# The projections of a second attention layer as products of rounded halves, with their weights streamed, in a fused two-layer kernel

## The chip, the cores and the metric

One core of one Trainium2 chip runs the whole program. The metric is the time of one execution on the device, in microseconds (us), of that core.

## The reference

Four batch rows of 512 tokens and width 256 pass through two layers, each a gated cross-attention and a gated feed-forward part. Only the second layer's attention matters here, cut from the reference:

```python
q = _split_heads(jnp.einsum('bnd,df->bnf', x, Wq))          # 16 heads of 64
kv = jnp.einsum('bmc,cf->bmf', context, Wkv)                # context 512 x 512
k, v = jnp.split(kv, 2, axis=-1)
nk = jnp.broadcast_to(null_kv[0], (b, HEADS, 1, DH))        # one null key for all
k = jnp.concatenate((nk, k), axis=-2)
attn = jax.nn.softmax(jnp.einsum('bhid,bhjd->bhij', q * scale, k), axis=-1)
out = jnp.einsum('bhij,bhjd->bhid', attn, v)
out = jnp.einsum('bnf,fd->bnd', out.transpose(0, 2, 1, 3).reshape(b, -1, INNER), Wout)
```

x is first normalised over its width; after the attention come a normalisation with scale and bias, the residual, and a mixture of eight experts of which each token uses two. All is in float32.

## The kernel before

The first layer fills the first third of the time, the second layer's attention (function `layer1`) the middle, the experts the rest. `layer1` walks over 32 groups, `i = 8 * b + p`: batch row b of four, and pair of heads p of eight (`PAIRS`). A group has four steps r = 0 to 3, one for each tile of 128 tokens or of 128 context rows. Every engine runs its own instructions in the order in which they are written, and semaphores join them.

In step (i, r) TensorE computes the scores of the next group (`scores(i + 1, r)`), transposes a quarter of this group's probabilities (`transpose_probs`, 8 transposes), and multiplies the quarter before it by the values (`weigh_values`). VectorE takes the row maxima of the new scores (`maxima`) and, one step later, divides the probabilities by their sums (`normalize`). ScalarE takes the exponentials (`exponentials`), copies the transposed probabilities out of PSUM (`keep_probs`) and the finished result (`keep_result`). The group's transposes start only when all four tiles of its probabilities are normalised (`p_ready`).

Into these steps a table, `slots`, puts further work, the fills. All fills share one PSUM bank, `MISC`, so a fill may start only when the one before it has been read out: `fill` waits for the reader's count, `misc_act` or `misc_dve`, and `read_fill` is that reader. The slot (i, r, 0) lies behind the scores and (i, r, 1) behind the transposes:

```python
        if 0 <= i + 2 < GROUPS:
            slots[i, 0, 0] = ("q", i + 2)
            slots[i, 1, 0] = ("k", i + 2)
```

A fill "q" projects the queries of a pair of heads (`project_queries`, 2 matmuls of 128x128 by 512 columns), "k" the keys (`project_keys`, 4 matmuls, two in step 1 and two in step 2), "v" a quarter of the values for half of the heads (`values`, 4 matmuls; 8 such fills for a batch row, in steps 3 of groups p = 0, 3, 4, 6, 7). "xT" transposes half of the next row's tokens (p = 5, in steps 2 and 3), "null" are the scores of the null key (p = 6, step 2, `null_scores`), "out" the output projection (p = 1, 2), "rT", "logits" and "prefix" belong to the choice of experts. `layer1` projects the keys and queries of groups 0 and 1 and the first values elsewhere; its own fills are 30 of q, 30 of k and 28 of v.

The projections are float32 matmuls. The scores are not: for groups 2 and later queries and keys are split when they are read out of PSUM into a part rounded to the format fp32r (`q_hi`, `k_hi`) and the remainder (`q_lo`, `k_lo`), and three fp32r matmuls, high by high, high by low and low by high, are added in PSUM. ScalarE rounds q, VectorE does the rest.

`wq`, `wk`, `wv` lie whole in SBUF, loaded once; the context of a batch row (`ctxT`) is loaded when the last keys of the row before are projected. The experts' weights will later stream into the SBUF buffers `w13_flat` and `w2_flat` of `Stream`; in the middle third these are empty until the last two groups. The trace calls the tiles of wq, wk, wv, ctxT and the experts' weights all `moe_w`, and xT `l_rows`. GpSimd adds a bias and a scale once per batch row and scatters rows for the experts.

## Time and profile before

| | |
|---|---|
| median of 3 runs | 1827.59 us (1826.96 to 1829.00) |
| the profiled execution's own time | 1830.33 us |
| its span, first to last instruction | 1828.6 us |
| mean granted clock of TensorE, as a share of 2.4 GHz | 0.983 |
| TensorE matmul busy, share of the span | 93% |
| VectorE, ScalarE, GpSimd busy | 65%, 57%, 21% |

Engines in the rows are PE (TensorE matmuls), PEld (its weight loads, which run beside them), DVE (VectorE), ACT (ScalarE), POOL (GpSimd) and SP (the queue that issues loads). A float32 matmul is two instructions in the trace. Matmuls are pipelined and their ends are modelled: the distance between starts is the cost of one, not its printed duration.

### The profile page before, as it was taken

To read this page: it belongs to the slowest core of one execution; us is meant where nothing else is said; L and a number is where in the kernel's file an instruction comes from. 1 tells how busy PE (TensorE), PEld (TensorE's weight loads), DVE (VectorE), ACT (ScalarE), POOL (GpSimd) and SP (SyncE) were. 2 spreads that over 40 slices of the span, in tenths; PEclk is the share of its full clock that TensorE was granted. 3 is DMA by queue.
4 is the path that set the end of the run, shared out by engine and by line. 5 is a ranking of instruction groups with operands and counts; after the bars stand their busy time and mean duration, and the time that the engine had idled before them with its cause. 6 is when DMAs were issued, how large, how long until landed. Compare 5 with 4: busy or idle time off the path is not lost.

```text
span 1828.6 us, 27461 instructions
## 1 busy us (share of the span) xinstructions
PE 1696.2 (93%) x9294; PEld 1082.1 (59%) x9294; DVE 1195.2 (65%) x2830; ACT 1045.7 (57%) x2160; POOL 375.5 (21%) x374
## 2 busy tenths in 40 slices
PE   5899998899799899999999999999998888999998
PEld 3455555455455345444554455444645788999997
DVE  3867876876778667555567457664676688666632
ACT  2467666666666656655555546555455466666621
POOL 2101110120011010000000000200021467777721
PEclk9899999999999999999999999999999899999999
DMA  3000000010003009200000000100001757777775
GB/s 104 1 24 1 1 24 1 1 28 3 1 1 138 2 2 347 73 24 1 1 1 23 1 1 1 58 2 1 13 25 56 227 148 218 214 210 198 218 230 161
DMA packets 121147, 127.10 MB, mean 70 GB/s; under 512 B 9904, under 2 KB 116400, under 8 KB 121008
## 3 DMA queue, kind: packets, MB, share of 16 engines
q1 hardware_dynamic: 113280, 116.68, 20.2%
q0 software_dynamic: 7152, 8.66, 2.6%
q8 instruction: 75, 1.23, 0.3%
q14 instruction: 64, 0.52, 0.1%
q10 hardware_dynamic: 576, 0.00, 0.0%
HBM read 96.46 MB, written 29.77 MB: 69 GB/s over the span
## 4 chain that ended last, share of the span: by engine, by line
PE 53%; DVE 5%; DVEq 1%; issue 1%; SPq 1%; ACT 0%; DMA 0%; POOLq 0%
PE psum L2497 8%; PE psum L1845 6%; PE psum L1716 6%; PE psum L1700 6%; PE psum L1722 5%; PE psum L1831 5%; PE psum L2515 4%; PE psum L1707 3%; PE psum L2472 3%; PE psum L1756 2%; PE psum L2482 1%; DVE moe_w_lo L2615 1%; DVE l_k_lo L2109 1%; DVE l_k_hi L2107 1%; PE psum L2454 0%
## 5 line engine op out<-in xcount | busy, mean ns | idle before, releaser
L1273 DVE TENSOR_REDUCE l_tile_max<-psum 128x1 f32<-128x512 f32 x512 | 342.1, 689 | 109.9 <-PE psum L951 108.2
L1121 ACT ACTIVATE l_probs<-psum 128x1024 f32<-128x1024 f32 x256 | 248.3, 1022 | 105.7 <-PE psum L963 102.0
L951 PE MATMUL psum<-l_kT,l_qT 128*128 128x512 f32 x512 | 238.3, 473 | 40.1 <-DVE l_tile_max L1273 36.8
L2049 DVE TENSOR_REDUCE l_row_max<-psum 128x2 f32<-128x1024 f32 x124 | 151.6, 1223 | 140.7 <-PE psum L1700 139.9
L2784 POOL TENSOR_TENSOR moe_w_lo<-moe_w,moe_w_hi 128x512 fp32r<-128x512 f32 x128 | 179.9, 1407 | 92.7 <-ACT moe_w_hi L2568 91.6
L951 PEld LDWEIGHTS psum<-l_kT,l_qT 128*128 128x128 f32 x512 | 98.0, 192 | 132.3 <-DVE l_tile_max L1273 111.7
L1888 ACT ACTIVATE l_probs<-psum,l_neg_max 128x512 f32<-128x512 f32 x248 | 167.2, 674 | 0.0
L963 PE MATMUL psum<-l_qT,l_kT 128*128 128x512 f32 x512 | 160.4, 397 | 1.7 <-ACT l_probs L1121 1.5
L1831 PEld LDWEIGHTS psum<-ident,l_probs 128*128 128x128 f32 x1024 | 120.5, 143 | 68.8 <-issue 53.1
L2599 ACT ACTIVATE moe_gate<-psum 128x256 f32<-128x256 f32 (+1 forms) x184 | 64.7, 352 | 158.7 <-PE psum L2497 98.5
L2497 PE MATMUL psum<-moe_xs_hi,moe_w_hi 128*128 128x256 f32 x512 | 148.0, 289 | 1.4 <-DVE moe_xs_lo L2625 1.4
L2497 PE MATMUL psum<-moe_xs_lo,moe_w_hi 128*128 128x256 f32 x512 | 146.3, 286 | 0.0
L2497 PE MATMUL psum<-moe_xs_hi,moe_w_lo 128*128 128x256 f32 x512 | 146.1, 285 | 0.0
L1831 PE MATMUL psum<-ident,l_probs 128*128 128x128 f32 x1024 | 136.3, 277 | 5.2 <-DVE l_probs L2063 3.9
L1845 PE MATMUL psum<-l_probsT,l_v_sb 128*64 128x512 f32 x512 | 140.6, 628 | 0.0
L978 PE MATMUL psum<-l_probs,l_v_ones 128*32 128x512 f32 x1024 | 138.7, 614 | 0.6 <-ACT l_probs L1121 0.6
L1886 ACT ACTIVATE l_null_p<-l_s_null,l_neg_max 128x1 f32<-128x1 f32 x248 | 71.4, 288 | 116.7 <-DVE l_neg_max L2051 116.4
L1926 ACT ACTIVATE l_probsT<-psum 128x1024 f32<-128x1024 f32 x128 | 130.4, 1019 | 5.7 <-PE psum L1831 5.7
L1716 PE MATMUL psum<-moe_w 128*128 128x512 f32 x240 | 119.0, 618 | 0.3 <-DVE router_work L545 0.3
L2063 DVE TENSOR_SCALAR l_probs<-l_probs,l_recip 128x512 f32<-128x512 f32 x248 | 110.0, 486 | 9.9 <-issue 0.4
L963 PEld LDWEIGHTS psum<-l_qT,l_kT 128*128 128x128 f32 x512 | 95.8, 189 | 29.4 <-ACT l_probs L1121 7.1
L1987 POOL TENSOR_TENSOR l_rows<-l_rows,l_ln_scale 128x256 f32<-128x256 f32 x12 | 9.8, 835 | 470.9 <-DVE l_rows L161 470.9
(361 smaller groups left out, 3278.6 us busy)
## 6 DMA issues: line engine op xcount, KB each, us to landing
moe_w<-in_moe_w SPq DMA_DIRECT2D x276, 256.0 KB, 4.6
moe_sorted_x<-l_null_cols SPq DMA_DIRECT2D x1, 17680.0 KB, 56.4
moe_xs<-moe_sorted_x SPq DMA_DIRECT2D x16, 272.0 KB, 2.9
moe_w<-in_ctx SPq DMA_DIRECT2D x8, 512.0 KB, 3.6
moe_w<-in_ctxT SPq DMA_DIRECT2D x4, 1024.0 KB, 5.7
moe_w<-in_wkv SPq DMA_DIRECT2D x2, 2048.0 KB, 15.7
x_resid<-in_x SPq DMA_DIRECT2D x4, 512.0 KB, 11.0
out_x<-x_resid SPq DMA_DIRECT2D x4, 512.0 KB, 4.4
```

The lines of the kernel that those rows point to most:

```text
L951: nc.tensor.matmul(bank(max_bank(m)), qT[:, q % SLOTS, h, t * P:(t + 1) * P], kT[:, q % SLOTS, h // 2, half * BANK:(half + 1) * BANK], sta ...
L963: last = nc.tensor.matmul(bank(2 * (n % 2) + i), kT[:, q % SLOTS, c, kt * P:(kt + 1) * P], qT[:, q % SLOTS, 2 * c + i, :], start=True, sto ...
L978: last = nc.tensor.matmul(bank(O_BANK)[32 * j:32 * j + 32, :], v_ones[:, q % SLOTS, kt, j, :], probs[:, (n + j // 2) % PT_RING, j % 2, :], ...
L1121: nc.scalar.activation(probs[:, n % PT_RING], wide(2 * (n % 2)), ACT.Exp, scale=SCALE).then_inc(exp_done, 1)
L1273: nc.vector.reduce_max(tile_max[:, q % 2, t, h, half:half + 1], bank(max_bank(m)), AX_X).then_inc(max_read, 1)
L1716: last = nc.tensor.matmul(bank(MISC), wk[:, c, p * P:(p + 1) * P], ctxT[:, c, :], start=(c == 0), stop=(c == s.CC - 1))
L1831: last = nc.tensor.transpose(bank(4 + j)[:, t * P:(t + 1) * P], probs[i % 2][:, t, j, kt * P:(kt + 1) * P], ident[:])
L1845: last = nc.tensor.matmul(bank(O_BANK)[j * DH:(j + 1) * DH, :], v_sb[:, kt, h * DH:(h + 1) * DH], probsT[:, m % 2, j, :], start=(kt == 0), ...
L1888: last = nc.scalar.activation(probs[i % 2][:, t, j, :], bank(2 * (t % 2) + j), ACT.Exp, bias=neg_max[:, t, j:j + 1], scale=SCALE, accum_ou ...
L2049: nc.vector.reduce_max(row_max[:, t, :], wide(2 * (t % 2)).rearrange("p (j m) -> p j m", j=2), AX_X)
L2497: last = nc.tensor.matmul(up_bank(k)[:, n * ROWS:(n + 1) * ROWS], w, x_part[:, i % 2, c, :], start=(c == 0 and j == 0), stop=(c == s.DC - ...
L2784: nc.gpsimd.tensor_tensor(w13_lo[:, at], w13[:, slot_k, :, cols], w13_hi[:, at].bitcast(F32), ALU.subtract).then_inc(w13_split, 1)
```

## The change

It concerns groups 8 to 31, batch rows 1 to 3. Their projections of q, k and v, and the null scores, are made from rounded halves, as the scores are: `product` issues three fp32r matmuls for each float32 one. Both operands must be split ahead:

- Weights: wq and wk come again from HBM in pieces of one pair's 128 columns, two groups ahead (`load_queries`, `load_keys`), the value weights in halves of 512 columns (`load_values`), all into the experts' empty buffers. ScalarE rounds the pieces of wq and wk (`round_queries` in step 2 for the group after the next but one, `round_keys` in step 0) and VectorE subtracts (`split_queries`, `split_keys`). GpSimd does both for the value weights (`split_values`, 4 copies and 4 subtractions of 128x512, six times).
- Context: it is loaded in two halves and split at p = 6, step 0, half before the maxima and half behind the reading of q (`round_context`, `split_context`). The tokens are split when they are read out of PSUM (ScalarE rounds, VectorE subtracts).
- Order: on TensorE the second half of a key projection moves ahead of the scores of step 2, and VectorE reads the keys ahead of that step's maxima. ScalarE copies the transposed probabilities (`keep_probs`) before it takes the exponentials of the step, in all 32 groups; except in step 3 it also reads a fill of slot 1 before them. In step 3 of p = 5 VectorE reads the tokens before it normalises.

```diff
     def is_split(fill):
-        return fill[0] in ("q", "k") and fill[1] >= 2
+        return fill[0] in ("q", "k") and fill[1] >= 2 or fill[0] == "xT" and fill[1] >= 1
...
+                for n in range(PAIRS - 1, GROUPS):
+                    b, p = divmod(n - 2, PAIRS)
+                    coming = (n + 1, n + 2) if n == PAIRS - 1 else (n + 2,) if n + 2 < GROUPS else ()
+                    sp.wait_ge(misc_psum, last_fill("q", n))
+                    for i in coming:
+                        load_queries(i)
+                    sp.wait_ge(misc_psum, last_fill("k", n))
+                    for i in coming:
+                        load_keys(i)
+                    if n % PAIRS == PAIRS - 1 and b + 1 < s.B:
+                        load_context(b + 1)
+                    if p == 0 and b >= 1:
+                        sp.wait_ge(misc_psum, last_fill("v", b, 0, KT - 1))
+                        load_values(1)
...
+                    if p == 4 and 1 <= b and b + 1 < s.B:
+                        sp.wait_ge(misc_psum, last_fill("v", b, 1, KT - 1))
+                        load_values(0)
...
+                def product(out, weights, moving, first, stop):
+
+                    terms = ((0, 0), (0, 1), (1, 0))
+                    for n, (x, y) in enumerate(terms):
+                        last = nc.tensor.matmul(out, weights[x], moving[y], start=(first and n == 0),
+                                                stop=(stop and n == len(terms) - 1))
+                    return last
...
+                    if i >= PAIRS:
+                        pe.wait_ge(wq_split, i - PAIRS + 1)
...
                     for r in range(4):
+                        if r == 2 and i + 2 < GROUPS:
+                            project_keys(i + 2, range(s.CC // 2, s.CC)).then_inc(misc_psum, 1)
                         if i + 1 < GROUPS:
                             scores(i + 1, r)
                         fill((i, r, 0))
-                        if r == 2 and i + 2 < GROUPS:
-                            project_keys(i + 2, range(s.CC // 2, s.CC)).then_inc(misc_psum, 1)
                         transpose_probs(i, r)
...
+                        if r == 0:
+                            round_soon(i)
                         read_fill((i, r, 0))
+                        if r == 0:
+                            round_rest(i)
+                        keep_probs(i, r)
+                        if r < 3:
+                            read_fill((i, r, 1))
                         if i + 1 < GROUPS:
                             exponentials(i + 1, r)
-                        keep_probs(i, r)
-                        read_fill((i, r, 1))
+                        if r == 3:
+                            read_fill((i, r, 1))
+                        if r == 2 and PAIRS <= i + 3 < GROUPS:
+                            round_queries(i + 3)
...
+                    for c in range(s.CC):
+                        nc.gpsimd.tensor_copy(wv_hi[:, c, :], wv_raw[:, c, :])
+                    pool.drain()
+                    for c in range(s.CC):
+                        nc.gpsimd.tensor_tensor(wv_lo[:, c, :], wv_raw[:, c, :], wv_hi[:, c, :].bitcast(F32),
+                                                ALU.subtract).then_inc(wv_split, 1)
...
+                def split_keys(i):
+                    dve.wait_ge(wk_rounded, i - PAIRS + 1)
+                    nc.vector.tensor_tensor(wk_lo[:, i % 2], wk_raw[:, i % 2], wk_hi[:, i % 2].bitcast(F32),
+                                            ALU.subtract).then_inc(wk_split, 1)
...
                 for i in range(GROUPS):
                     for r in range(4):
+                        if r == 0:
+                            split_soon(i)
+                        if r == 2:
+                            read_fill((i, 1, 0))
                         if i + 1 < GROUPS:
                             maxima(i + 1, r)
                         if r == 0:
                             read_fill((i, 0, 0))
-                        if r == 2:
-                            read_fill((i, 1, 0))
+                            split_rest(i)
```

Place one is TensorE in group 6, step 2, where the keys of group 8 are finished and the null scores of row 1 follow. In the kernel before (L1700 scores, L1716 keys, L1831 transposes, L1736 null scores, L1845 values weighed; the float32 matmul is one row here):

```order
L1700 MATMUL psum<-l_k_hi,l_q_hi 128x512 x2
L1700 MATMUL psum<-l_k_lo,l_q_hi 128x512 x2
L1700 MATMUL psum<-l_k_hi,l_q_lo 128x512 x2
L1716 MATMUL psum<-moe_w 128x512 x2
L1831 MATMUL psum<-ident,l_probs_52 128x128 x8
L1736 MATMUL psum<-l_w_null,l_rows 128x16 x8
L1845 MATMUL psum<-l_probsT,l_v_sb 64x512 x2
```

and in the changed kernel (L1771 is `product`, L1763 the scores, L1926 the transposes):

```order
L1771 MATMUL psum<-l_ctx_hi,l_wk_hi 128x512
L1771 MATMUL psum<-l_ctx_lo,l_wk_hi 128x512
L1771 MATMUL psum<-l_ctx_hi,l_wk_lo 128x512
L1771 MATMUL psum<-l_ctx_hi,l_wk_hi 128x512
L1771 MATMUL psum<-l_ctx_lo,l_wk_hi 128x512
L1771 MATMUL psum<-l_ctx_hi,l_wk_lo 128x512
L1763 MATMUL psum<-l_k_hi,l_q_hi 128x512 x2
L1763 MATMUL psum<-l_k_lo,l_q_hi 128x512 x2
L1763 MATMUL psum<-l_k_hi,l_q_lo 128x512 x2
L1926 MATMUL psum<-ident,l_probs_52 128x128 x8
```

Two float32 matmuls have become six fp32r ones, and they stand before the scores; behind the transposes now come 24 small matmuls of the null scores in place of 8.

Place two is ScalarE from step 3 of a group with two value fills to step 0 of the next. Before (L1908 reads values, L1886 and L1888 are the exponentials, L1926 copies transposed probabilities, L1902 rounds q, L1934 keeps the result):

```order
L1908 ACTIVATE l_v_sb<-psum 128x512
L1886 ACTIVATE l_null_p<-l_s_null,l_neg_max 128x1
L1888 ACTIVATE l_probs,l_p_sum<-psum,l_neg_max 128x512
L1886 ACTIVATE l_null_p<-l_s_null,l_neg_max 128x1
L1888 ACTIVATE l_probs,l_p_sum<-psum,l_neg_max 128x512
L1926 ACTIVATE l_probsT<-psum 128x1024
L1908 ACTIVATE l_v_sb<-psum 128x512
L1902 ACTIVATE l_q_hi<-psum 128x512
```

and in the changed kernel (L2003 values, L2047 the copy, L1981 and L1983 the exponentials):

```order
L2019 ACTIVATE l_wq_hi<-moe_w 128x256
L2003 ACTIVATE l_v_sb<-psum 128x512
L2047 ACTIVATE l_probsT<-psum 128x1024
L1981 ACTIVATE l_null_p<-l_s_null,l_neg_max 128x1
L1983 ACTIVATE l_probs,l_p_sum<-psum,l_neg_max 128x512
L1981 ACTIVATE l_null_p<-l_s_null,l_neg_max 128x1
L1983 ACTIVATE l_probs,l_p_sum<-psum,l_neg_max 128x512
L2003 ACTIVATE l_v_sb<-psum 128x512
L2023 ACTIVATE l_wk_hi<-moe_w 128x512
L1997 ACTIVATE l_q_hi<-psum 128x512
L2047 ACTIVATE l_probsT<-psum 128x1024
```

The copy now stands ahead of the exponentials, and two roundings of weights have come in.

Place three is VectorE in steps 1 and 2 of a group. Before (L2049, L2051 maxima, L2057 to L2063 normalising, L2107, L2109 keys):

```order
L2049 TENSOR_REDUCE l_row_max<-psum 128x2
L2051 SCALAR_TENSOR_TENSOR l_neg_max<-l_row_max,l_s_null 128x2
L2107 CAST l_k_hi<-psum 128x512
L2109 TENSOR_TENSOR l_k_lo<-psum,l_k_hi 128x512
L2057 TENSOR_TENSOR l_denom<-l_p_sum,l_null_p 128x2
L2059 RECIPROCAL l_recip<-l_denom 128x2
```

and in the changed kernel:

```order
L2249 CAST l_k_hi<-psum 128x512
L2251 TENSOR_TENSOR l_k_lo<-psum,l_k_hi 128x512
L2191 TENSOR_REDUCE l_row_max<-psum 128x2
L2193 SCALAR_TENSOR_TENSOR l_neg_max<-l_row_max,l_s_null 128x2
L2199 TENSOR_TENSOR l_denom<-l_p_sum,l_null_p 128x2
L2201 RECIPROCAL l_recip<-l_denom 128x2
L2205 TENSOR_SCALAR l_probs_52<-l_probs_52,l_recip 128x512 x2
L2268 TENSOR_TENSOR l_wq_lo<-moe_w,l_wq_hi 128x256
```

The reading of the keys has moved ahead of the maxima, and a subtraction for the query weights follows the step.

## Rows read from the trace of the kernel before

**Rows 1.** Stretch: length, busy PE, PEld, DVE, ACT, POOL (instructions), clock, DMA share, GB/s

```profile
684.00:1426.00 742.00, 722.55 (x3316) 380.61 (x3316) 450.94 (x1191) 410.98 (x1017) 48.81 (x75) 0.99 0.14 43
```

**Rows 2.** Waits of PE in 684 to 1426 us: total us, times, longest

```profile
PE psum L1831 <- DVE l_probs L2063: 3.9, 3, 3.0
...
PE psum L1736 <- DVE l_k_lo L2109: 2.0, 3, 0.7
```

**Rows 3.** Timeline of PEld from 1013 us, value fill: start, us

```profile
1013.88 0.19 PEld L1722 LDWEIGHTS psum<-moe_w 128*128 128x128 f32 x1 [0.28 <-issue]
...
1016.02 0.19 PEld L1722 LDWEIGHTS psum<-moe_w 128*128 128x128 f32 x1 [0.24 <-issue]
```

**Rows 4.** Groups by line, all of the kernel: xcount, busy us, mean ns

```profile
L1716 PE MATMUL psum<-moe_w 128*128 128x512 f32 x240 | 119.0, 618 | 0.3 <-DVE router_work L545 0.3
L1722 PE MATMUL psum<-moe_w 128*128 128x512 f32 x224 | 103.0, 602 | 0.0
L1707 PE MATMUL psum<-l_rows,moe_w 128*128 128x512 f32 x120 | 59.5, 618 | 0.0
```

**Rows 5.** Chain that ended last, pieces: start, us

```profile
896.25 3.46 PE psum L1756 x16
1007.15 1.96 PE psum L1736 x16
1660.21 1.44 PE psum L2497 x12
```

**Rows 6.** Timeline of PE from 1018 us: start, us

```profile
1018.32 0.39 PE L1700 MATMUL psum<-l_k_lo,l_q_hi 64*128 64x512 f32 x2
1018.55 0.40 PE L1700 MATMUL psum<-l_k_hi,l_q_lo 64*128 64x512 f32 x2
1018.88 1.98 PE L1707 MATMUL psum<-l_rows,moe_w 128*128 128x512 f32 x4
1020.70 1.04 PE L1831 MATMUL psum<-ident,l_probs 128*128 128x128 f32 x8
1021.66 1.08 PE L1845 MATMUL psum<-l_probsT,l_v_sb 128*64 128x512 f32 x4
```

**Rows 7.** Groups by line: reading, maxima, exponentials, copies

```profile
L2049 DVE TENSOR_REDUCE l_row_max<-psum 128x2 f32<-128x1024 f32 x123 | 150.4, 1223 | 139.1 <-PE psum L1700 138.2
L2109 DVE TENSOR_TENSOR l_k_lo<-psum,l_k_hi 128x512 fp32r<-128x512 f32 x30 | 20.8, 692 | 2.2
L506 DVE TENSOR_TENSOR router_tied<-router_tie,router_lower_expert 128x256 f32<-128x256 f32 x3 | 1.3, 426 | 0.2
L1926 ACT ACTIVATE l_probsT<-psum 128x1024 f32<-128x1024 f32 x128 | 130.4, 1019 | 5.7 <-PE psum L1831 5.7
```

**Rows 8.** Timeline of ACT and DVE from 738 us: one pair of exponentials, then normalising

```profile
738.42 0.29 ACT L1886 ACTIVATE l_null_p<-l_s_null,l_neg_max 128x1 f32<-128x1 f32 x1 [1.96 <-DVE l_neg_max L2051]
740.13 1.01 ACT L1926 ACTIVATE l_probsT<-psum 128x1024 f32<-128x1024 f32 x1
740.27 0.16 DVE L2057 TENSOR_TENSOR l_denom<-l_p_sum,l_null_p 128x2 f32<-128x2 f32 x1 [0.61 <-ACT l_probs L1888]
741.54 1.22 DVE L2049 TENSOR_REDUCE l_row_max<-psum 128x2 f32<-128x1024 f32 x1
```

**Rows 9.** Groups by line in the experts' part: rounding and subtracting

```profile
L2568 ACT ACTIVATE moe_w_hi<-moe_w 128x512 fp32r<-128x512 f32 x128 | 80.8, 631 | 0.0
L2615 DVE TENSOR_TENSOR moe_w_lo<-moe_w,moe_w_hi 128x256 fp32r<-128x256 f32 x128 | 81.6, 639 | 0.1
```

**Rows 10.** Groups by line of POOL

```profile
L2784 POOL TENSOR_TENSOR moe_w_lo<-moe_w,moe_w_hi 128x512 fp32r<-128x512 f32 x128 | 179.9, 1407 | 92.7 <-ACT moe_w_hi L2568 91.6 <-issue 0.2
L1250 POOL COPY l_rows<-l_rows 128x512 f32<-128x512 f32 x16 | 10.3, 644 | 53.3 <-DVE l_rows L1298 53.3
```

**Rows 11.** DMA issues: KB each, median us to landing

```profile
moe_w<-in_ctxT SPq DMA_DIRECT2D x4, 1024.0 KB, 5.7
```

**Rows 12.** A stretch around the null scores of row 1, same columns as rows 1

```profile
820.00:826.00 6.00, 6.00 (x34) 4.41 (x34) 2.69 (x7) 0.71 (x3) 0.00 (x0) 0.72 0.00 0
```

More of the change, by code:

```diff
@@ L1625, in layer1 @@
         q_rounded = sem("l1_q_rounded")
+        xT_rounded = sem("l1_xT_rounded")
+        wq_in = [sem(f"l1_wq_in_{i}") for i in range(2)]
+        wq_rounded = sem("l1_wq_rounded")
+        wq_split = sem("l1_wq_split")
+        wk_in = [sem(f"l1_wk_in_{i}") for i in range(2)]
+        wk_rounded = sem("l1_wk_rounded")
+        wk_split = sem("l1_wk_split")
+        wv_in = sem("l1_wv_in")
+        wv_split = sem("l1_wv_split")
+        ctx_in = [sem(f"l1_ctx_in_{i}") for i in range(2)]
+        ctx_rounded = sem("l1_ctx_rounded")
+        ctx_split = sem("l1_ctx_split")
+        w_null_split = sem("l1_w_null_split")
         null_cols_ready = sem("l1_null_cols_ready")
@@ L1733, in null_scores @@
                 def null_scores(b):
+                    if b == 1:
+                        pe.wait_ge(w_null_split, 1)
                     for t in range(T):
+                        some = slice(t * P, (t + 1) * P)
                         for c in range(s.DC):
-                            last = nc.tensor.matmul(bank(MISC)[:, t * H:(t + 1) * H], xT[:, c, t * P:(t + 1) * P],
-                                                    w_null[:, c, :], start=(c == 0), stop=(c == s.DC - 1))
+                            last = product(bank(MISC)[:, t * H:(t + 1) * H], (xT_hi[:, c, some], xT_lo[:, c, some]),
+                                           (w_null_hi[:, c, :], w_null_lo[:, c, :]), c == 0, c == s.DC - 1)
                     return last
@@ L1893, in read_fill @@
                 def read_fill(at):
-                    if at not in slots or read_by_dve(slots[at]) and slots[at][0] != "q":
+                    if at not in slots or read_by_dve(slots[at]) and slots[at][0] not in ("q", "xT"):
                         return
@@ L1909, in read_fill @@
                     elif kind == "xT":
-                        last = nc.scalar.activation(xT[:, rest[1], :], bank(MISC), ACT.Copy)
+                        nc.scalar.activation(xT_hi[:, rest[1], :], bank(MISC), ACT.Copy).then_inc(xT_rounded, 1)
+                        return
                     elif kind == "w_null_v":
```

145 lines of the change are left out of this document (127 added, 18 removed).

## The prediction

> **What bounds the kernel now.** I read the stretches first, to find where the changed part lies and which engine fills it. From 684 to 1426 us, the second layer's attention, the matmul row is busy 722.6 of 742 us at a clock of 0.99, VectorE 451 and ScalarE 411 us [rows 1]. Since that row is modelled, I then asked the waits. TensorE's are few: 3.9 us for normalised probabilities, and four rows alike, 2.0 us each in three waits, on the remainder of the keys (`l_k_lo`, L2109), where a fill in slot 1 of step 2 stands behind the keys in the same PSUM bank (null scores, first tokens, null columns, first router tokens) [rows 2]. So TensorE sets the pace of this stretch, group after group, and what its instructions lose in length the kernel gains, until another chain takes over. The timeline then gives the distances between starts.
>
> **What the products save.** Inside a value fill the float32 instructions start (1016.02 - 1013.88) / 5 = 0.428 us apart [rows 3]; a float32 matmul of 512 columns is two of them, 0.856 us. The trace has 240 + 224 + 120 = 584 such instructions for keys, values and queries, 292 matmuls [rows 4]. Batch row 0 keeps its own: 6 pairs by 2 and by 4, and 4 value fills by 4, 52 matmuls. That leaves 240 to change: 24 groups by 2 and by 4, and 24 value fills by 4. They take 205.4 us now and become 720 fp32r matmuls.
>
> No row shows an fp32r matmul of 128 rows by 512 columns. The bounds:
> - Below: half of a float32 instruction's pace. 512 columns in 0.428 us for a pass at two slots per column is 0.214 us for 512 slots.
> - Above: twice the 256-column fp32r matmul of the experts, 12 in 1.44 us, 0.12 each [rows 5], so 0.24.
> - Between: the scores, two heads side by side with two weight loads per start, 1018.55 - 1018.32 = 0.23 [rows 6]; and the float32 instructions of 256 columns, 16 in 3.46 us, 0.216 each, which have the same 512 slots and one load of 128x128 each [rows 5].
>
> I take 0.216, because that row has the array time and the one weight load of the new matmul, while 0.12 looks like a matmul shorter than its weight load. 720 x 0.216 = 155.5 us: **-49.9 us**. At 0.214 it would be -51.3, at 0.23 -39.8, at 0.24 -32.6.
>
> The trace's 0.216 is weighed against a rule here. The Trainium skill (TensorE: Matmul & The Clock Gate, Wait - 56ns, not 53.3ns?) says that warm matmuls start N / 2.4 GHz plus about 2.5 ns apart, 215.7 ns for 512 columns; by that the term would be -50.1, and the trace agrees within 0.001 us. The same page (Back-to-back issue gap) gives about 131 ns for a sustained stream at 512 columns; by that 720 matmuls would take 94 us and the term would be -111. This trace's streams of 256 columns at 0.12 us and of 512 slots at 0.216 us speak against it.
>
> The null scores grow from 16 records to 24 matmuls, three times. They move hardly any columns: 16 in 1.96 us, 0.12 each [rows 5]. 24 more cost **+2.9 us**. Around them the granted clock falls, 0.72 over 820 to 826 us [rows 12], between its levels of 1.2 and 2.4 GHz, after TensorE had done small matmuls. I give the longer stretch 0.5 us each, **+1.5 us**; bounds are nothing and 1.7 us each, since 28% of those 6 us was lost.
>
> **What the new order saves.** The keys are now finished before the scores of step 2 and read before its maxima. From their end TensorE has scores (0.89 us with its boundary) and transposes (1020.70 to 1021.66, 0.96) to do [rows 6], 1.85 us, and VectorE needs two instructions of 0.69, 1.4 us [rows 7]. The four rows of waits go: 4 x 2.0 = **-8.0 us**. If VectorE came late to the keys, nothing would be gained; that is the other bound.
>
> **What the new order costs.** The group's transposes wait for the last tile's exponentials and their division. Before, these began with the maxima, beside the transposes; now ScalarE first copies. From the end of the last scores: transposes 0.96, copy 1.02 [rows 7], exponentials 1.71 (738.42 to 740.13), normalising 1.27 (740.27 to 741.54) with 0.14 between [rows 8], together 5.1 us. TensorE meanwhile has transposes 0.96, weighing 1.01, scores 0.89 and a query block, 1.82 before [rows 6] and 1.4 now: 4.3 us, or 4.7 with float32 queries. Where step 3 holds a value, an output or another long fill (over 2.7 us), nothing shows. It shows in groups 0 and 2, 0.4 us each, and in p = 5 of rows 0 to 2, 0.8 plus a rounding of query weights in front (0.4, between nothing and the 0.63 of a rounding twice as wide [rows 9]): **+4.4 us**. Bounds: nothing, and 1.2 us in all 30 groups, 36 us (a rival).
>
> **What the splits cost.** VectorE: its two-input instructions are 0.426 us for 256 elements and 0.692 for 512 [rows 7], so 0.27 per 256 more. Keys 0.69 and queries 0.43 in 24 groups, context halves 1.22 and tokens 0.69 six times: 38 us on 451. ScalarE: at most 0.63 twice in 24 groups, context 1.02 six times: 36 us on 411. In a stretch of about 698 us they would be busy 70% and 64%, and TensorE's work hides them. Where that cover fails is step 0 of p = 6: key weights and half a context (1.9 us) stand before the maxima (1.22) and the reading of q (0.69), 3.8 us after scores that VectorE reaches about a microsecond late; TensorE is at the next key fill, which needs q read, 1.4 + 0.96 + 1.01 + 0.89 = 4.3 us after those scores. I put 1.2 us in three places, estimated from the difference with the wake-ups between three engines: **+3.6 us**, from nothing to 2.5 each.
>
> GpSimd: 4 copies of 0.644 and 4 subtractions of 1.407 us [rows 10], 8.2 us six times. A half is loaded at least two groups, some 40 us, before its values, and 1024 KB land in 5.7 us [rows 11]; so TensorE doesn't wait for it. But beside GpSimd's subtractions in the experts' part VectorE takes 0.639 us for 256 elements [rows 9], alone 0.426 [rows 7]: half as much again. Six times 8.2 us with VectorE busy 0.65 are 32 us of its work, 16 us more at worst; VectorE has 30% idle, and I take **+2 us**, from nothing to 16. The Trainium skill (GPSIMD Engine Reference, Specifications) says why it speaks against this change: the two engines share their SBUF interfaces, with contention for VectorE instructions that have two SBUF inputs or run in a two-port mode. The trace agrees, with 0.639 against 0.426 us.
>
> The loads are small and early: a piece of wq or wk is asked for two groups ahead. ScalarE's roundings wait for them, with everything of ScalarE behind.
>
> **The sum.** -49.9 + 2.9 + 1.5 - 8.0 + 4.4 + 3.6 + 2 = -43.5 us. The profiled execution took 1830.3 us (1828.6 span), 2.7 above the median of its runs; 1830.3 - 43.5 = 1786.8, less 2.7: **1784 us**.
>
> **The rivals.**
> - *All as planned, without new waits.* The last four costs vanish (11.5 us) and the pace is 0.214: 1771 us. For it: VectorE and ScalarE have a third of the time free [rows 1]. Against: the 5.1 against 4.3 us above. Chance 0.10.
> - *The fp32r matmul is slower than its slots*, 0.24 us with its loads, as the experts' [rows 5]: the saving is 32.6, 17 less: 1801 us. For it: 0.23 in the scores [rows 6]. Chance 0.12.
> - *Another chain becomes the bound.* Copy, exponentials and division, or VectorE beside GpSimd, hold TensorE 1.2 us in some 26 groups: 31 us back, 1815 us. For it: the chain is already the longer one where no fill helps; against: 19 of 24 changed groups have a long fill in step 3. Chance 0.12.
> - *The other side: the streamed pieces come late.* ScalarE waits at the head of step 0 for key weights, and behind it stand the reading of q, the copy and the exponentials. It decides from 43.5 / 24 = 1.8 us per group; at 4 us in each the kernel takes 1784 + 96 = 1880 us. Against: 5.7 us for 1024 KB [rows 11], and this stretch uses 14% of the DMA [rows 1]; the pieces have rows of only 512 bytes, which no row here prices. Chance 0.04.
> - Chains and lateness together just eat the gain: 0.02.
>
> The forecast itself has 0.60, with a range of its own from 1775 to 1796. Two in ten are left out below 1767 (where all bounds would help) and above 1806 (most of the third rival, all of the fourth), so the range is 1767 to 1806. About 0.2%, 3.7 us, is what a measurement of this kernel can tell from no change. Faster 0.94, within it 0.02, slower 0.04.
>
> **What would show it.** The stretch of 742 us ends about 43 us earlier, the first layer and the experts' part as long as before. In a value fill `product` instructions start 0.216 us apart. The waits of PE lose the four rows on `l_k_lo`; waits of the transposes on `l_probs` grow from 3.9 to about 8 us. VectorE is busy 38 us more there, ScalarE up to 36, GpSimd 49. I am wrong if the products start 0.23 or more apart, if the transposes wait for copies or probabilities in most groups, or if ScalarE's roundings wait on DMA.

## The result, and the profile after

The changed kernel takes 1819.89 us (median of 5 runs, 1817.35 to 1821.98), the kernel before, run beside it, 1827.59 us (1825.88 to 1829.43): a ratio of 0.995, with an interval from 0.9937 to 0.9964. So it is faster by 7.7 us in the medians and 9 by the ratio, where 43.5 were forecast, and lies above the range.

The stretch of the second layer's attention, same columns as [rows 1]:

```profile
684.00:1426.00 742.00, 706.66 (x3609) 436.72 (x3609) 506.86 (x1275) 446.97 (x1082) 98.08 (x126) 0.97 0.22 68
```

VectorE is busy 55.9 us more than in [rows 1] (forecast 38), ScalarE 36.0 (up to 36), GpSimd 49.3 (49). The granted clock is 0.97 instead of 0.99. The waits of TensorE in this stretch, which answer to [rows 2]:

```profile
PE psum L1926 <- DVE l_probs L2205: 7.5, 6, 5.3
PE psum L1822 <- DVE l_xT_lo L2254: 5.8, 3, 2.7
PE psum L1771 <- ACT l_v_sb L2003: 3.8, 2, 2.0
PE psum L1822 <- DVE l_k_lo L2251: 2.4, 2, 1.6
PE psum L1771 <- DVE l_q_lo L2245: 2.2, 3, 0.7
PE psum L1771 <- DVE l_k_lo L2251: 2.1, 2, 1.0
PE psum L1868 <- DVE l_k_lo L2251: 1.9, 1, 1.9
```

The regular rows on `l_k_lo` (three times 0.7 each) are gone, as forecast, but fewer and longer ones stand in their place, and a new row, the second transposed tokens waiting for the remainder of the first (`l_xT_lo`). Waits of 1.6 to 2.7 us in single places are the sign to follow. (The 5.3 us on `l_probs` stand in group 30, where TensorE waited 3.0 before.)

A query block in the new form (timeline of TensorE), which answers to [rows 6]:

```profile
1018.97 0.50 PE L1771 MATMUL psum<-l_xT_hi,l_wq_hi 128*128 128x512 f32 x1
1019.31 0.40 PE L1771 MATMUL psum<-l_xT_lo,l_wq_hi 128*128 128x512 f32 x1
1019.54 0.39 PE L1771 MATMUL psum<-l_xT_hi,l_wq_lo 128*128 128x512 f32 x1
1019.77 0.40 PE L1771 MATMUL psum<-l_xT_hi,l_wq_hi 128*128 128x512 f32 x1
1020.01 0.39 PE L1771 MATMUL psum<-l_xT_lo,l_wq_hi 128*128 128x512 f32 x1
1020.24 0.39 PE L1771 MATMUL psum<-l_xT_hi,l_wq_lo 128*128 128x512 f32 x1
1020.47 1.03 PE L1926 MATMUL psum<-ident,l_probs 128*128 128x128 f32 x8
```

The products start 0.23 us apart, not 0.216, and the first of a block stands 0.34 ahead of the second.

**Where the time went.** Step lengths show it best. I take them from the trace as distances between the starts of successive blocks of weighted values (L1845 before, L1940 after): per group the rest of step 2, step 3, then steps 0 and 1 of the next group. "Before", "after" and four of the experiments below, us:

```
                        before                 e3 orders only         after
group  7 (row 0, p 7)   4.70  9.93 4.70 4.69   4.84 9.92 4.70 4.69    4.51 8.57 4.36 4.36
group 13 (row 1, p 5)   6.04  3.36 5.33 4.69   5.28 3.36 6.55 4.69    6.82 7.02 5.31 5.18
group 14 (row 1, p 6)   7.32  7.94 4.69 4.70   6.54 6.36 4.69 4.69    8.71 8.50 4.36 4.39

                        e4 no GpSimd split     e5 VectorE eased       e7 everything eased
group  7                4.51  8.56 4.36 4.36   4.51 8.57 4.36 4.36    4.52 8.57 4.36 4.36
group 13                4.96  5.80 5.71 5.18   6.75 4.25 5.30 5.18    4.95 4.31 5.31 5.83
group 14                9.85  7.36 4.36 4.36   7.09 7.21 4.36 4.39    7.10 5.90 4.36 4.36
```

Group 7 is what the middle of a row looks like: 24.02 us became 21.80. Groups 13 and 14, where the next row's tokens and contexts are prepared, went from 44.07 to 50.28. Summed over the 31 groups between the first weighted values and those of group 31: 718.24 before, 706.84 after, 11.4 less.

This is the end of that row in the changed kernel, VectorE, GpSimd and two of TensorE's waits (timeline):

```profile
974.47 0.16 DVE L2193 SCALAR_TENSOR_TENSOR l_neg_max<-l_row_max,l_s_null 128x2 f32<-128x2 f32 x1
974.52 5.36 POOL L2169 TENSOR_TENSOR l_wv_lo<-moe_w,l_wv_hi 128x512 fp32r<-128x512 f32 x4
974.55 1.25 DVE L2199 TENSOR_TENSOR l_denom<-l_p_sum,l_null_p 128x2 f32<-128x2 f32 x1
976.12 2.62 DVE L2205 TENSOR_SCALAR l_probs<-l_probs,l_recip 128x512 f32<-128x512 f32 x2
978.66 1.69 DVE L161 TENSOR_SCALAR l_rows<-x_resid,l_mv,l_work 128x256 f32<-128x256 f32 x2
981.77 0.66 PE L1822 MATMUL psum<-ident,l_rows 128*128 128x128 f32 x4 [1.64 <-DVE l_k_lo L2251]
983.61 0.88 DVE L2205 TENSOR_SCALAR l_probs<-l_probs,l_recip 128x512 f32<-128x512 f32 x2
984.94 1.41 DVE L76 BATCH_NORM_STATS2 l_stats<-x_resid 128x6 f32<-128x256 f32 x4 [0.44 <-issue]
986.26 0.67 DVE L2254 TENSOR_TENSOR l_xT_lo<-psum,l_xT_hi 128x512 fp32r<-128x512 f32 x1
986.99 0.75 PE L1822 MATMUL psum<-ident,l_rows 128*128 128x128 f32 x4 [2.66 <-DVE l_xT_lo L2254]
```

Read it from the left: while GpSimd subtracts (974.52 to 979.88), a pair of normalising instructions takes 2.62 us, and 0.88 when GpSimd is still. VectorE then comes late to the keys, TensorE waits 1.64. Behind that stand a tile's work and routing statistics of another row, 1.41 us, ahead of the token remainder, and TensorE waits 2.66. What the granted clock does is in the windows, same columns as [rows 1]; the first begins at the end of the wait, the second at the end of the null scores (1005.50 to 1008.57), ahead of which TensorE had waited 1.03 us:

```profile
987.00:991.00 4.00, 4.00 (x16) 2.34 (x16) 3.68 (x12) 2.11 (x4) 0.00 (x0) 0.57 0.00 0
1008.00:1015.00 7.00, 7.00 (x26) 4.38 (x26) 3.83 (x11) 1.90 (x5) 0.00 (x0) 0.52 0.01 4
```

TensorE is at its lower level, 1.2 GHz, for 3.4 us in the first window and 6.7 in the second. Summing windows of one microsecond over the 31 groups gives 16.9 us at that level before and 40.7 after; at half speed they cost up to 8 and 20 us.

### The profile page after: what moved, and what is told of

Its sections match the earlier page's. It is cut to its first block and busy times, and to the rows that moved or that the text cites. A ratio compares the mean times of both kernels' runs of the same rounds, so it can differ in the third digit from the quotient of the medians.

```text
span 1818.2 us, 28277 instructions
## 1 busy us (share of the span) xinstructions
PE 1675.6 (92%) x9558; PEld 1135.1 (62%) x9558; DVE 1244.6 (68%) x2892; ACT 1076.3 (59%) x2214; POOL 421.2 (23%) x422
## 5 line engine op out<-in xcount | busy, mean ns | idle before, releaser
L2047 ACT ACTIVATE l_probsT<-psum 128x1024 f32<-128x1024 f32 x128 | 131.1, 1024 | 140.2 <-PE psum L1926 135.1
L2191 DVE TENSOR_REDUCE l_row_max<-psum 128x2 f32<-128x1024 f32 x124 | 151.0, 1218 | 35.5 <-PE psum L1763 35.0
L1983 ACT ACTIVATE l_probs<-psum,l_neg_max 128x512 f32<-128x512 f32 x248 | 168.3, 679 | 0.0
L1926 PEld LDWEIGHTS psum<-ident,l_probs 128*128 128x128 f32 x1024 | 121.1, 146 | 45.6 <-issue 24.7
L1926 PE MATMUL psum<-ident,l_probs 128*128 128x128 f32 x1024 | 141.9, 284 | 7.6 <-DVE l_probs L2205 7.5
L1940 PE MATMUL psum<-l_probsT,l_v_sb 128*64 128x512 f32 x512 | 143.9, 641 | 0.0
L2205 DVE TENSOR_SCALAR l_probs<-l_probs,l_recip 128x512 f32<-128x512 f32 x248 | 120.2, 527 | 9.9 <-issue 0.4
L2952 DVE TENSOR_TENSOR psum<-psum,moe_gate 128x256 f32<-128x256 f32 x128 | 54.7, 428 | 74.1 <-ACT moe_gate L2788 74.0
L2686 PEld LDWEIGHTS psum<-moe_xs_hi,moe_w_hi 128*128 128x128 f32 x512 | 99.9, 195 | 1.8 <-DVE moe_xs_lo L2814 1.8
L2686 PEld LDWEIGHTS psum<-moe_xs_lo,moe_w_hi 128*128 128x128 f32 x512 | 99.8, 195 | 0.0
```

Source lines behind the costliest of these rows:

```text
L1926: last = nc.tensor.transpose(bank(4 + j)[:, t * P:(t + 1) * P], probs[i % 2][:, t, j, kt * P:(kt + 1) * P], ident[:])
L1940: last = nc.tensor.matmul(bank(O_BANK)[j * DH:(j + 1) * DH, :], v_sb[:, kt, h * DH:(h + 1) * DH], probsT[:, m % 2, j, :], start=(kt == 0), ...
L1983: last = nc.scalar.activation(probs[i % 2][:, t, j, :], bank(2 * (t % 2) + j), ACT.Exp, bias=neg_max[:, t, j:j + 1], scale=SCALE, accum_ou ...
L2047: nc.scalar.activation(probsT[:, m % 2], wide(4).rearrange("p (j n) -> p j n", j=2), ACT.Copy).then_inc(pT_ready, 1)
L2191: nc.vector.reduce_max(row_max[:, t, :], wide(2 * (t % 2)).rearrange("p (j m) -> p j m", j=2), AX_X)
L2686: last = nc.tensor.matmul(up_bank(k)[:, n * ROWS:(n + 1) * ROWS], w, x_part[:, i % 2, c, :], start=(c == 0 and j == 0), stop=(c == s.DC - ...
```

## The experiments

Each kernel ran 4 to 12 times beside the kernel before; e4 and e8 leave work out, so e4's values are not the reference's and e8's are less exact. "31 groups" is the sum above and "low" the time at the lower clock in it, both from the profiled execution.

```
kernel                       median us   ratio to before [95%]       31 groups  low
before                                                                 718.2   16.9
after                        1819.89     0.995  [0.9937, 0.9964]       706.8   40.7
e1 exponentials first        1833.37     1.0025 [1.0008, 1.0042]       718.4   37.5
e2 keys behind the scores    1831.95     1.0014 [1.0003, 1.0024]       717.6   44.3
e3 before, new orders only   1822.78     0.996  [0.9947, 0.9973]       711.2    6.8
e4 no split by GpSimd        1805.96     0.9887 [0.9871, 0.9903]       694.9   20.3
e5 VectorE's order eased     1805.77     0.9868 [0.985, 0.9886]        691.3   23.9
e6 values by ScalarE/VectorE 1816.12     0.9917 [0.9898, 0.9936]       698.5   30.7
e7 everything eased          1799.02     0.9832 [0.9812, 0.9852]       683.7   10.2
e8 two products of three     1770.54     0.9685 [0.9667, 0.9704]       657.2   27.2
e9 e3 with statistics later  1821.13     0.9957 [0.9942, 0.9973]       708.7    6.7
e10 e7, context split back   1802.21     0.9863 [0.9843, 0.9883]       686.8   10.2
e11 e10, mixed orders        1803.06     0.9858 [0.9839, 0.9877]       688.0   13.5
e12 e7, mixed orders         1800.04     0.9837 [0.9822, 0.9853]       681.2   10.2
```

The theories: **A**, the new orders took back the gain. **B**, product pace and low clock did, whatever the orders. **C**, GpSimd's split slows VectorE by more than was allowed for. **D**, VectorE is full where a row ends, and is the chain that binds there.

One thing stands across these theories. In the profiled executions of the changed kernel, of e4, e10 and e11 ScalarE stalls in groups 20 and 28 and TensorE with it (groups of 25.34 and 23.86 us after the change); in those of e5, e6, e7 and e12 TensorE loses nothing there (21.7 to 22.2 us each), for no reason that a run shows. That is 5.5 us of the 31 groups between the changed kernel and e5, e6 or e7, and it is taken off below where two such kernels are compared.

### The orders: e1, e2, e3

e1, ScalarE:

```
-keep_probs(i, r)
-if r < 3: read_fill((i, r, 1))
 if i + 1 < GROUPS: exponentials(i + 1, r)
-if r == 3: read_fill((i, r, 1))
+keep_probs(i, r)
+read_fill((i, r, 1))
```

> The changed kernel with ScalarE's order in a step put back: exponentials, then the copy of the probabilities, then the middle bank. Theory A (the part of the gain that is missing went to the new orders): the copy first delays the exponentials and so VectorE's last normalisation and the next transposes; put back, 4 to 10 us come back (1810 to 1816). Theory B (it went to product pace and to low clock after single long waits, for which the order is not to blame): within 3 us of the changed kernel (1817 to 1823), or slower, since the weighted values then wait for the copy again.

e2, on TensorE and in the same way on VectorE (keys read behind the maxima):

```
-if r == 2 and i + 2 < GROUPS: project_keys(i + 2, range(s.CC // 2, s.CC))
 if i + 1 < GROUPS: scores(i + 1, r)
 fill((i, r, 0))
+if r == 2 and i + 2 < GROUPS: project_keys(i + 2, range(s.CC // 2, s.CC))
```

> The changed kernel with the second half of the key projection back behind the scores, and VectorE's reading of the keys back behind the maxima. The half ahead of the scores costs TensorE one boundary more of 0.15 us in 30 groups, 4.5 us; behind them the keys are read later, and the waits on the key remainder (8.0 us of before, 6.4 us of after) may return. Theory A (orders): 1 to 5 us faster than the changed kernel (1815 to 1819). Theory B: no difference to 4 us slower (1820 to 1824), since waits and low clock take the place of the boundaries.

e3 is the kernel before with the reverse of both edits.

> The kernel before, its float32 projections kept, with the new orders alone: keys' second half ahead of the scores and read ahead of the maxima, and ScalarE's copy of the probabilities ahead of the exponentials. Theory A (orders cost): 5 to 12 us slower than before (1833 to 1840). Theory B: within 4 us of before (1824 to 1832): 8 us of waits on the key remainder go, 4.5 us of boundaries and some waits on the probabilities come.

Theory A falls three times. Each order put back costs more than the whole gain (ratios 1.0025 and 1.0014), and the orders alone, without a single new product, give 0.996: about 7 us, nearly as much as the whole change measures. What the orders are good for shows in TensorE's waits of e1, in the changed kernel's stretch:

```profile
PE psum L1926 <- ACT l_probsT L2047: 13.8, 13, 1.9
PE psum L1822 <- DVE l_xT_lo L2251: 9.3, 3, 3.3
PE psum L1771 <- ACT router_rT L2012: 3.8, 2, 1.9
```

and of e2:

```profile
PE psum L1926 <- DVE l_probs L2205: 10.2, 8, 5.4
PE psum L1822 <- DVE l_k_lo L2251: 7.1, 3, 3.1
PE psum L1771 <- DVE l_k_lo L2251: 6.3, 4, 2.6
PE psum L1868 <- DVE l_k_lo L2251: 4.9, 2, 3.3
```

With shorter blocks TensorE comes sooner to what it waits for; the exponentials in front of the copy, or the keys behind the maxima, are then late by more than before the change. e2 also confirms the price of the half ahead: 4.36 us for the rest of step 2 in group 7, where it is 4.51 with the half ahead. That is the extra block boundary, 0.15 us in 30 groups, 4.5 us that the forecast did not have.

### GpSimd: e4 and e6

e4 leaves the split out; the value products take `wv_hi` in place of `wv_lo`:

```
-for c in range(s.CC): nc.gpsimd.tensor_copy(wv_hi[:, c, :], wv_raw[:, c, :])
-pool.drain()
-for c in range(s.CC): nc.gpsimd.tensor_tensor(wv_lo[:, c, :], wv_raw[:, c, :], ..., ALU.subtract).then_inc(wv_split, 1)
+if b == 1 and half == 0:
+    for c in range(s.CC): nc.gpsimd.tensor_copy(wv_hi[:, c, :], wv_raw[:, c, :])
+nc.gpsimd.tensor_copy(wv_lo[:, 0, 0:64], wv_raw[:, 0, 0:64]).then_inc(wv_split, s.CC)
```

> The changed kernel without GpSimd's splitting of the value weights: it rounds the first half once, and then only a 64-column copy per half signals TensorE; the value products take the rounded weights in place of the remainders, so the number of products, the loads and everything else stay, and the values are not the reference's. Theory C (VectorE beside GpSimd is slowed by more than the 2 us of the prediction): waits on the probabilities, on the transposed tokens and on the keys shrink, and with them low clock: 6 to 15 us faster than the changed kernel (1805 to 1814). Theory B (pace and other waits): within 3 us of it.

The ratio goes from 0.995 to 0.9887, 11.5 us, and the 31 groups from 706.8 to 694.9. Both kernels have the stall, so this difference is free of it. Between the same blocks VectorE is busy 495.7 us in the changed kernel and 475.9 in e4. The groups of VectorE's normalising, after and in e4, up to 1390 us:

```profile
L2205 DVE TENSOR_SCALAR l_probs<-l_probs,l_recip 128x512 f32<-128x512 f32 x246 | 119.3, 527 | 9.8 <-issue 0.4
```

```profile
L2204 DVE TENSOR_SCALAR l_probs<-l_probs,l_recip 128x512 f32<-128x512 f32 x248 | 110.0, 486 | 9.9 <-issue 0.4
```

A mean of 527 against 486 ns looks harmless, but it hides two populations. Sorted by whether one of GpSimd's subtractions runs at the same time, the changed kernel's instructions are:

```
VectorE instruction, ns, 684 to 1390 us       not beside   beside L2169
l_probs, one input, SBUF to SBUF (L2205)      486          1329 (12 of them)
l_neg_max, two inputs (L2193)                 168           816 (5)
l_rows, layer norm applied (L161)             447          1364 (2)
l_row_max, from PSUM (L2191)                  1218         1218 (4)
l_k_lo, one input from PSUM (L2251)           692           692 (1)
l_recip (L2201)                               166           166 (6)
```

The slow ones are slower by up to about the length of a subtraction (1.36 us), whatever their own size; the two kinds that read PSUM don't notice, and neither does the reciprocal. Taken over every VectorE instruction that runs beside a subtraction, what they take above the median of their own kind adds up to 17.4 us. GpSimd's copies disturb less: 1.9 us in all, most of it in `l_rows`, 0.690 us beside a copy (5 of them) against 0.406 with GpSimd still. The Trainium skill (SBUF — State Buffer, Who interferes with whom) calls it an exclusive lock: whichever of the two engines issues first holds the shared ports for its whole instruction, and for VectorE it concerns two-port modes and instructions with two SBUF inputs. This trace agrees for the two-input kind, with 0.17 against 0.82 us. For the one-input kind, 0.49 against 1.33, it fits, but whether that ran in a two-port mode isn't in the trace. The "half as much again" that the forecast took from the experts' part would be an average over such cases.

But e4 still has the wait at the row's end:

```profile
976.13 1.40 DVE L76 BATCH_NORM_STATS2 l_stats<-x_resid 128x6 f32<-128x256 f32 x4 [0.44 <-issue]
977.45 0.67 DVE L2253 TENSOR_TENSOR l_xT_lo<-psum,l_xT_hi 128x512 fp32r<-128x512 f32 x1
978.18 0.66 PE L1822 MATMUL psum<-ident,l_rows 128*128 128x128 f32 x4 [2.37 <-DVE l_xT_lo L2253]
```

e6 gives the split to ScalarE (`activation` into `wv_hi`, a piece in each of four steps) and VectorE:

```
+SPLIT_AT = (((5, 3), (6, 1), (6, 2), (6, 2)), ((1, 3), (1, 3), (2, 3), (2, 3)))
+nc.vector.tensor_tensor(wv_lo[:, c, :], wv_raw[:, c, :], wv_hi[:, c, :].bitcast(F32), ALU.subtract).then_inc(wv_split, 1)
```

> The changed kernel with the value weights split by ScalarE (the rounding, four pieces of a half in four steps) and VectorE (the remainder, four pieces of 0.69 us), and none by GpSimd: the same numbers come out. Theory C: the 12 to 14 us that came with GpSimd's split left out come here too, less what 28 VectorE pieces (19 us of work, partly in full steps) cost: 1810 to 1816. Theory D: VectorE's pieces in pairs 5 and 6 lengthen what is full already; 1816 to 1825.

Its ratio is 0.9917: of 11.5 us only 6 come, and in the 31 groups 8.4 us, of which 5.5 are the stall, so about 3 of e4's 12. Groups 14 and 22 take 28.18 and 26.54 us there, 25.96 and 25.98 in the changed kernel. C is right about GpSimd, and D says why its work can't simply move to VectorE.

### VectorE where a row ends: e5, e7, e9

e5 keeps GpSimd's split and moves nothing but three pieces of VectorE's work:

```
 normalize(i + 1, r - 1)
+if tokens_soon: read_fill((i, 2, 1))      # first xT_lo ahead of the extras
 extra(*divmod(i, PAIRS), r)
...
-route_at = 16 if soon else 22
+route_at = 16 if soon else 26             # statistics in steps 26 to 28, tokens in 29
```

> The changed kernel with VectorE's order eased where a row ends: in step 2 of pair 5 the remainder of the first transposed tokens is taken ahead of the routing statistics, and those statistics and the routed tokens move by four steps, from pairs 5 and 6 to pairs 6 and 7. GpSimd splits the value weights as before. Theory D (VectorE, full in pairs 5 and 6, is the chain that binds there, and TensorE's low clock follows its waits): the steps of groups 13, 14, 21 and 22 shrink by 1 to 3 us each, 5 to 12 us faster than the changed kernel, 1810 to 1817 beside a kernel before of 1828. Theory C (GpSimd's contention alone does it): within 3 us of the changed kernel, and the same waits elsewhere.

The ratio is 0.9868, 15 us below the changed kernel, 15.5 in the 31 groups. Group 13 takes 21.5 us instead of 24.3, group 14 23.1 instead of 26.0, and groups 13, 14, 21 and 22 together 9.6 less. The wait that had been 2.7 us at its longest:

```profile
PE psum L1822 <- DVE l_xT_lo L2254: 2.9, 3, 1.2
```

The rest of e5's gain is not from there: ScalarE's stall in group 20 (below) is missing, 3.5 us with the low clock behind it, and 2.0 in group 28. Without it the move is worth about 10 us, within D's 5 to 12, and near e4's 12 with all of GpSimd's split gone.

e7 puts e5 and e6 together and spreads the context split:

```
 def split_soon(i):
-    if p == 6 and b + 1 < s.B: split_context(b + 1, 0)
...
 if r == 0:
     read_fill((i, 0, 0))
-    split_rest(i)
+if r < 2:
+    split_rest(i, r)                       # half r of the context, in pair 6
...                                        # and the same for ScalarE's rounding
```

> The two runs above together, and the context split spread: its first half behind the query remainder, its second in step 1 of pair 6. Theory D with C: no GpSimd beside VectorE and the full steps eased, 15 to 25 us faster than the changed kernel (1795 to 1805 beside a kernel before of 1828). If product pace and low clock without a cause in VectorE explain the missing gain: 1806 or more.

1799.02 us, ratio 0.9832, 31 us below the kernel before. The place that took 2.66 us, VectorE and TensorE:

```profile
982.07 0.88 DVE L2215 TENSOR_SCALAR l_probs<-l_probs,l_recip 128x512 f32<-128x512 f32 x2
982.87 0.68 DVE L2264 TENSOR_TENSOR l_xT_lo<-psum,l_xT_hi 128x512 fp32r<-128x512 f32 x1
983.61 0.66 PE L1837 MATMUL psum<-ident,l_rows 128*128 128x128 f32 x4 [0.88 <-DVE l_xT_lo L2264]
```

and a window over the null scores that follow, same columns as [rows 1]:

```profile
998.00:1005.00 7.00, 7.00 (x52) 5.13 (x50) 5.71 (x16) 4.62 (x14) 0.00 (x0) 1.00 0.12 37
```

The 24 small matmuls whose end the changed kernel's window at 0.52 begins with stand whole in this one (1000.55 to 1003.31), and the clock is 1.00, and stays there behind them. So null scores alone needn't lower it. But the waits alone don't decide it either. In row 0 (group 6) it falls in both kernels, and in e5 it falls in all three rows, though TensorE's last wait stands 7 us ahead of the null scores (0.75 us at 993.58), where e7 waited longer (1.44 at 993.78). The window behind e5's null scores in group 14:

```profile
1003.00:1007.00 4.00, 4.00 (x17) 2.09 (x17) 2.63 (x7) 0.71 (x3) 0.00 (x0) 0.59 0.02 6
```

Why the clock fell there and not in e7 stays open.

e9 is e3 with one more edit, so the float32 projections with the orders and the later statistics:

```
-route_at = 16 if soon else 22
+route_at = 16 if soon else 26
```

> The kernel before with the three new orders and the routing statistics four steps later, float32 projections kept: what the easing is worth without the new projections. Step 0 of pair 6 in groups 13 and 21 took 6.55 us with the orders alone, where 5.3 would do. If VectorE is full at a row's end only because of the new splits: within 3 us of the orders alone (1820 to 1824 beside a kernel before of 1829). If it is full anyway: 1815 to 1819.

It has 0.9957, e3 has 0.996: the easing is worth nothing measurable before the splits come. Its group 13 does lose the 6.55 us step (5.30). Against e9, e7 is 0.0125 lower, 23 us: that is what the new projections are worth with the work around them put where there is room (in e9 TensorE loses nothing in groups 20 and 28 either).

### The price of a product: e8

```
-terms = ((0, 0), (0, 1), (1, 0))
+terms = ((0, 0), (0, 1))
```

> The changed kernel with the third of the three products left out (weights' remainder by rounded data), in the projections and null scores; all loads, splits and waits stay, the output is not the reference's to full accuracy. 240 products of 512 columns fewer. If TensorE binds nearly everywhere and a product is 0.228 us: 55 us faster than the changed kernel, 1765. If another chain binds from here on: only 20 to 40 us faster (1780 to 1800), with waits on the probabilities in most groups.

1770.54 us, a ratio of 0.9685: 48 us for 240 products of 512 columns and 24 small ones. Group 7 goes from 21.80 to 18.64 us with 14 products fewer, 0.226 each. TensorE binds where the row is even; what is short of 54 (240 x 0.226) is in the ends of the rows, where waits grow:

```profile
PE psum L1822 <- DVE l_xT_lo L2254: 7.1, 3, 3.6
PE psum L1771 <- ACT l_v_sb L2003: 6.1, 9, 1.3
```

### The rest of the way: e10, e11, e12

e10 is e7 with this undone:

```
-if r < 2: split_rest(i, r)
+if r == 0: split_rest(i)
```

> The run with everything eased, but the context split where the changed kernel has it, both halves in step 0 of pair 6. With its second half in step 1, step 1 of pair 6 took 5.83 us, where 5.18 was seen with both in step 0, in three rows. If that wait is all that the move did: 2 us faster, 1794 to 1799; if the first half ahead of the maxima delays the null scores again, with low clock behind them: up to 10 us slower, 1800 to 1808.

The median, 1802.21, lies in the second theory's 1800 to 1808, but not for its reason. Step 1 of pair 6 hardly changed (5.78 for 5.83), the null scores neither. The difference to e7, 3.1 us in the 31 groups, is in groups 20 and 28, 2.0 and 1.7 us: a stall of ScalarE while GpSimd scatters rows, here with TensorE behind it.

```profile
1145.29 1.08 POOL L2180 DMA_INDIRECT moe_sorted_x<-router_rows,router_slot_ids  x1 [0.30 <-issue]
1146.67 0.97 POOL L2180 DMA_INDIRECT moe_sorted_x<-router_rows,router_slot_ids  x1 [0.30 <-issue]
1148.85 1.02 ACT L2067 ACTIVATE l_probsT<-psum 128x1024 f32<-128x1024 f32 x1 [3.62 <-remote]
1152.12 0.50 PE L1786 MATMUL psum<-l_xT_hi,l_wq_hi 128*128 128x512 f32 x1 [1.91 <-ACT l_v_sb L2018]
```

The DMA queues from 1146 to 1150 us in the same kernel:

```profile
q0 software_dynamic: 102, 0.28, 20.6%
q14 instruction: 1, 0.01, 0.8%
```

The changed kernel has the same stall at 1157 to 1161 us, 3.57 us long. It comes and goes between kernels whose ScalarE programs have the same instructions (e7 and e10). A fetch of instructions (q14) held up behind the scatter would look like this, but no run moved the scatter, so that stays a reading.

e11 and e12 put ScalarE's exponentials first in pair 6 of the last row. e11 also has them first in step 0 of groups 1 to 3; e12 instead has the keys' half behind the scores in pairs 2 to 4.

```
+copy_first = i != GROUPS - 2
+behind = i % PAIRS in (2, 3, 4)
```

> As the run before this, with ScalarE's exponentials ahead of the copy in two places alone: in step 0 of pairs 1 to 3 of the first row, and in pair 6 of the last row. There the copy-first order cost 0.4 to 0.6 us a step and about 2 us (group 30: 18.3 us with the exponentials first, 21.0 with the copy first). If each place acts by itself: 3 to 5 us faster than the run before this one. If the waits move to the steps behind: within 1 us of it.

> The run with everything eased (1799 beside a kernel before of 1830), with each old order kept where it was seen to be the better one: the second half of the keys behind the scores, and read behind the maxima, in pairs 2, 3 and 4 (4.36 us a step where it is 4.52 with the half ahead), and ScalarE's exponentials first in pair 6 of the last row (18.7 us for the group where it is 21.0). If each place acts by itself: 12 times 0.15 and 2.3 us, 4 us faster, 1793 to 1797. If the waits move: 1798 to 1801. A 3.6 us stall of ScalarE near the scatter of the rows, in some kernels there and in some not, would hide the difference.

Group 30 takes 18.7 us in e11, where it took 21.0; but the steps of row 0 stay at 5.30 (in e1, which has the exponentials first in every step, they are 4.69; so the exponentials that delay step 0 are likely those of step 3 before it, and the edit was in the wrong place), and the stalls in groups 20 and 28 cost 2 and 3.6 us. e12 wins its 0.15 us in nearly every group of pairs 2 to 4 and 1.3 in group 30, 2.5 in all in the profiled execution; the ratios, 0.9837 and 0.9832, tell nothing apart. e7 and e12 are the best versions, 1.7 and 1.6% below the kernel before, and both beat the changed kernel by over 1%.

## Why the forecast was wrong, step by step

- **Products.** The mechanism was right, the price mis-sized. Group 7 of e9 takes 24.15, of e7 21.82: 2.33 us for 14 replaced matmuls, 0.166 each instead of 0.208; for 240 that is -39.9, where -49.9 stood. That is the bound given for 0.23 us (-39.8). The row of scores, 0.23, was the right neighbour, and not the float32 instructions of 256 columns at 0.216. At 0.226 us (e8) the products run 5% slower than the 215.7 ns that the Trainium skill (TensorE: Matmul & The Clock Gate, Wait - 56ns, not 53.3ns?) gives for 512 columns, and far from the 131 ns of its Back-to-back issue gap. This is the second rival at little more than half its price: 10 us, where it had 17, of the 32 that are missing in the 31 groups (43.5 forecast, 11.4 measured).
- **Waits on the keys, and the chain copy, exponentials, division.** -8.0 + 4.4 = -3.6 forecast; e3 has -7.0 in the 31 groups. Right in direction, and better by up to 5 us because there was less low clock too (16.9 to 6.8 us); the extra boundary of 4.5 us was not in the sum. The costs in groups 0 and 2 came as worked out (step 0 of the next group, 4.88 to 5.30); group 1 has one too (4.69 to 5.30), for which the forecast had nothing.
- **VectorE beside GpSimd, +2.** This step failed most clearly. The subtractions added 17.4 us to VectorE's work, about the 16 that stood as the worst case (e4 has 19.8 less between the same blocks); and the argument that 30% idle time hides it was an average over groups. Without the split 11.5 us come back (e4), where 2 were allowed for. The 55.9 us in the fixed window can't be compared with the forecast's 38 directly, since the faster kernel has got 11 us further in it; between the same blocks VectorE's work grew by 49.4, and by 29.6 without GpSimd's split (e4).
- **Null scores, clock and step 0 of pair 6, +2.9 +1.5 +3.6.** The null scores were priced right: 24 products took 2.76 us in e7, where 16 records had taken 1.96, so 2.4 us in three rows. Step 0 of pair 6 was not late: 5.31 us after, 5.33 before. The late places are steps 2 and 3 of pair 5, where the forecast costed only the chain, and where the token remainders (0.69 us each) stand behind another row's statistics, and the same steps of pair 6 behind them. e5 shows it: three pieces of VectorE's work moved, about 10 us without the stall.
- **The sum of these last four.** After e3, the changed kernel gains 4.4 us in the 31 groups instead of 39.9: 35.5 us of costs, where 10.0 were forecast. Of them 23 go with e7 (5.5 of these are ScalarE's stall, which the forecast didn't have and no edit explains), 12 are left there. By another count up to 17 are low clock (40.7 against 6.8 us at half speed) and 14 are TensorE's waits over 0.15 us (29.9 against 15.9 us in all, ten of them over 1 us). That the low clock comes from the waits is a reading: in the changed kernel it came with four of the five waits of 1.8 to 2.7 us, but also in row 0, and in e5, without one. No run changed the clock alone, so that cause stays open.
- **Rivals.** The third, another chain bound, was the right one with the wrong place: it spoke of 26 groups, and it is four or five steps at each row's end, each dearer. Streamed pieces were never late: no rounding of ScalarE waited for a DMA. The measured time lies near that rival's 1815, by other places and prices, so the nearness of the number is luck.
- The text ahead of the prediction says that the experts' weight buffers are empty in the middle of the kernel. They aren't: they hold the second layer's projection weights and the context there, whole in the kernel before; the change puts its streamed pieces and split parts in these places.

## What to carry to other kernels

A third of idle time on an engine hides nothing in the steps where its work is bunched: lay out the few steps in which a row, a tile or a phase ends, and check the order on each engine there before adding to it. Moving three pieces of VectorE's work was worth about 10 us here, the whole change 9. And take an unseen instruction's price from the row of the same data type, even when another row has the same columns.

## What the hardware showed beyond that

- Some VectorE instructions beside a GpSimd subtraction with two SBUF inputs are longer by up to about all of it: 0.486 against 1.329 us in 12 cases, 0.168 against 0.816 in 5; from PSUM 1.218 against 1.218, and the reciprocal 0.166 against 0.166.
- fp32r products of 128 rows by 512 columns with a weight load each: 0.226 to 0.23 us apart, and some 0.11 us more at a block's first.
- In the changed kernel TensorE was at 1.2 GHz for 3.4 us behind waits of 1.85, 2.29 and 2.66 us (from 1164.9, 1182.0 and 987.4), for 6.8 us behind one of 1.87 (1076.2), and in e5 for 3.4 us behind 24 small matmuls with no wait in the 7 us ahead of them.
- ScalarE stalled 1.5 to 3.7 us in groups 20 or 28, near a scatter by GpSimd, in eight of the kernels, and up to 8.4 us in group 31, on nothing that the program names.
